# A two-layer transformer kernel: combining, gathers and routing of the last stage in another order, key weights folded into the query weights, and a straight TensorE program

## The reference, cut to what matters

```python
x = _layernorm(x + _L0_ffn_ref(...))           # its gather and sum are the "combine" of stage C
# layer 1, attention
Q = X @ W_q + b_q;  K = X @ W_k + b_k;  V = X @ W_v + b_v
A = softmax(einsum('bsd,btd->bst', Q, K) * scale, axis=2)
x = _layernorm(x + einsum('bst,btv->bsv', A, V))
# layer 1, feed-forward: 8 small experts, 2 of them per row, from the better of 2 groups
scores = sigmoid(xf @ gate.T);  sfc = scores + corr_bias
group_scores = top_k(sfc.reshape(N, 2, 4), 2)[0].sum(-1)     # sum of the two largest of four
sfc = sfc masked to the better group;  sel = top_k(sfc, 2)[1]
top_scores = scores[sel] / (scores[sel].sum(-1) + 1e-20)
lat = xf @ fc1_w.T
out_e = relu2(lat @ w1[e].T) @ w2[e].T;  comb = sum over e of out_e * top_scores
shared = relu2(xf @ up_w.T) @ down_w.T
x = _layernorm(x + comb @ fc2_w.T + shared)
```

## Time and profile before

| | before |
|---|---|
| time, median of 3 runs | 2147.3 us (2143.82 to 2147.42) |
| time of the profiled execution | 2149.05 us |
| its span (first to last record) | 2147.3 us |
| mean granted TensorE clock | 0.948 of full speed |
| busy of the span: PE, DVE, ACT, POOL | 90%, 67%, 41%, 33% |
| stage C: first q product of the 8 batches | 825.21, 987.93, 1151.72, 1318.39, 1483.74, 1649.88, 1816.66, 1978.68 us |

### The profile page before, as it was taken

The page is one execution under the profiler, slowest core; times in us unless marked ns, Lnnn a source line. Parts: engine busy times, 40 slices in busy tenths (PEclk is TensorE's granted clock), DMA queues, the critical chain, the costliest instruction groups (busy, mean ns, idle before and its releaser), DMA issues.

```text
span 2147.3 us, 36004 instructions
## 1 busy us (share of the span) xinstructions
PE 1926.1 (90%) x11720; PEld 1685.6 (79%) x11752; DVE 1433.3 (67%) x3448; ACT 880.3 (41%) x1580; POOL 707.5 (33%) x611
## 2 busy tenths in 40 slices
PE   7999899259999957999999999999999989989997
PEld 6888787249999956878888878877877977978976
DVE  4778887434434535786785785785786786687666
ACT  3344444232323314345344444344444434444433
POOL 4145555510000022253253254244145145145033
PEclk9999899679999987999999999999999999999999
DMA  4322222032223321021121111112112112111011
GB/s 148 152 96 96 95 97 65 25 118 79 88 78 109 114 93 42 29 80 48 33 80 41 40 62 59 38 42 80 32 48 81 30 50 81 26 55 50 11 40 60
DMA packets 92613, 144.54 MB, mean 67 GB/s; under 512 B 14543, under 2 KB 72743, under 8 KB 91569
## 3 DMA queue, kind: packets, MB, share of 16 engines
q1 hardware_dynamic: 79120, 110.99, 15.2%
q0 software_dynamic: 13344, 31.64, 5.4%
HBM read 103.21 MB, written 48.79 MB: 71 GB/s over the span
## 4 chain that ended last, share of the span: by engine, by line
PE 38%; DVE 13%; issue 6%; ACT 3%; POOL 2%; DVEq 0%; DMA 0%; ACTq 0%; POOLq 0%
PE c_ps L118 8%; PE c_ps L120 8%; PE c_ps L119 8%; PE c_ps L127 3%; PE c_ps L128 3%; PE c_ps L129 2%; PE c_ps L1693 2%; POOL c_place L1283 2%; DVE c_shared_place L1618 2%; DVE c_key L97 1%; DVE c_tmp L97 1%; PE c_ps L1754 1%; DVE c_place L1538 1%; PE c_ps L1756 1%; PE c_ps L1755 1%
## 5 line engine op out<-in xcount | busy, mean ns | idle before, releaser
L1283 POOL TENSOR_TENSOR c_place<-c_shared_place,c_place 128x512 fp32r<-128x512 f32 x256 | 328.6, 1307 | 387.7 <-DVE c_shared_place L1618 228.5
L118 PE MATMUL c_ps<-c_place 128*128 128x256 f32 (+1 forms) x768 | 250.8, 327 | 6.1 <-DVE c_place L1538 6.1
L1274 POOL DMA_INDIRECT c_gathered<-expert_results,c_slots x112 | 112.6, 1006 | 417.1 <-DVE c_pre L1467 396.8
L120 PE MATMUL c_ps<-c_place 128*128 128x256 f32 (+1 forms) x768 | 245.3, 319 | 0.0
L119 PE MATMUL c_ps<-c_place 128*128 128x256 f32 (+1 forms) x768 | 244.5, 318 | 0.0
L1618 DVE SCALAR_TENSOR_TENSOR c_shared_place<-c_ps,c_shared_place 128x512 f32<-128x512 f32 x256 | 170.1, 682 | 31.7 <-ACT c_shared_place L1413 31.6
L127 PE MATMUL c_ps<-c_downT_hi,c_place 128*128 128x256 f32 x512 | 152.8, 298 | 18.6 <-POOL c_place L1283 18.6
L118 PEld LDWEIGHTS c_ps<-c_place 128*128 128x128 f32 x768 | 146.1, 190 | 18.0 <-DVE c_place L1538 7.9
L1421 ACT ACTIVATE c_place<-c_shared_place 128x512 fp32r<-128x512 f32 x128 | 80.3, 630 | 188.9 <-DVE c_shared_place L1618 187.9
L120 PEld LDWEIGHTS c_ps<-c_place 128*128 128x128 f32 x768 | 146.0, 190 | 11.0
L119 PEld LDWEIGHTS c_ps<-c_place 128*128 128x128 f32 x768 | 146.3, 190 | 10.4
(11 more groups left out here) (345 smaller groups left out, 5638.1 us busy)
## 6 DMA issues: line engine op xcount, KB each, us to landing
c_x2T<-score_rows SPq DMA_DIRECT2D x64, 512.0 KB, 5.3
a_xT_raw<-xT SPq DMA_DIRECT2D x8, 1024.0 KB, 6.5
a_x_rows<-x SPq DMA_DIRECT2D x8, 1024.0 KB, 5.1
x_rows<-a_x SPq DMA_DIRECT2D x8, 1024.0 KB
c_pre<-x_rows SPq DMA_DIRECT2D x8, 1024.0 KB, 5.5
out<-c_x SPq DMA_DIRECT2D x16, 512.0 KB, 3.0
expert_rows<-a_zeros POOLq DMA_DIRECT2D x7, 1024.0 KB, 14.3
b_win_raw<-w_in SPq DMA_DIRECT2D x7, 1024.0 KB, 7.8
```

What stands on the lines that cost most here:

```text
L118: pe.matmul(out, lh, rh, start=(j == 0), stop=False)
L120: last = pe.matmul(out, ll, rh, start=False, stop=(j == len(terms) - 1))
L1274: pool.indirect_dma_start(rows[:, a, :], None, d["ys"], bass.IndirectOffsetOnAxis(ap=slots[:, a, t:t + 1], axis=0), bounds_check=TRASH + P ...
L1283: pool.tensor_tensor(hid_lo[:, place, :], square[:, place % RING, :], f32(hid_hi[:, place, :]), ALU.subtract).then_inc(hid_split, 1)
```

## The change

In **stage C** the key product goes: `Wq·Wkᵀ` is made once, ahead of the batches, and called `wqk`; `q` is then `x·wqk`, and `score` multiplies it with the rows `x2T` themselves. The part of the key bias that does not cancel in the softmax comes out of two extra columns of `v` (258 instead of 256) as `row_bias`, one small DVE operation for each `v` unit (line 1575 of the kernel after) and another behind each maximum (line 1584). A `v` unit now takes two banks. The next batch's combining moves from the attention into the part of the expert units. `GATHER` goes from 2 to 4, and POOL issues four tiles' gathers at the start of its batch and the other four between its splits of the first half. The route chain has 27 operations instead of 31, two of them without a wait. `gate 0` and `gateT 0` stand one `mix` earlier, `mix 7` and `ln3 1` stand behind `up (0, 0)` and `up (0, 1)`, and `x3T 1` behind `expert (0, 0)`. ACT's copies `norm_x2` stand in the last two expert units. TensorE's loop over batches 1 to 6 becomes a Python loop: its program is written out six times, and the other engines' loops stay. In **stage A** `slots` moves to the end of the list. In **stage B** `wq` and `wk` are not loaded or split there any more; they are loaded at the start of stage C. Cut to its core, the diff is:

```diff
-             ("proj", 1), ("logitT", 0), ("vk", 0), ("vk", 1), ("q", 0), ("q", 1), ("mixT", 1), ("q", 2), ("slots", 0), ("q", 3),
-             ("split", 0), ("copy", 0), ("proj", 2), ("proj", 3)]
+             ("proj", 1), ("logitT", 0), ("vk", 0), ("vk", 1), ("q", 0), ("q", 1), ("mixT", 1), ("q", 2), ("q", 3),
+             ("split", 0), ("copy", 0), ("proj", 2), ("proj", 3), ("slots", 0)]
...
-             ("score", 7), ("mix", 5), ("turn", 6), ("x3T", 0), ("combine", 4), ("mix", 6), ("turn", 7), ("gate", 0), ("combine", 5),
-             ("gateT", 0), ("mix", 7), ("ln3", 1), ("latent", 0), ("up", (0, 0)), ("scoreT", 0), ("combine", 6), ("norm3", 1),
-             ("combine", 7), ("up", (0, 1)), ("ln2", 0), ("x3T", 1), ("expert", (0, 0)), ("gate", 1), ("expert", (0, 1)), ("gateT", 1),
-             ("comb", 0), ("up", (1, 0)), ("scoreT", 1), ("out", 0), ("latent", 1), ("up", (1, 1)), ("ln4", 0), ("expert", (1, 0)),
...
+             ("latent", 0), ("up", (0, 0)), ("mix", 7), ("scoreT", 0), ("up", (0, 1)), ("ln3", 1), ("norm3", 1), ("combine", 0),
+             ("expert", (0, 0)), ("x3T", 1), ("combine", 1), ("gate", 1), ("expert", (0, 1)), ("combine", 2), ("combine", 3), ("gateT", 1),
+             ("comb", 0), ("combine", 4), ("up", (1, 0)), ("combine", 5), ("scoreT", 1), ("out", 0), ("latent", 1), ("combine", 6),
+             ("up", (1, 1)), ("combine", 7), ("ln2", 0), ("ln4", 0), ("expert", (1, 0)), ("expert", (1, 1)), ("comb", 1),
+             ("x2T", 0), ("x2T", 1), ("out", 1)]
...
+    V_COUNT = {"q": 1, "v": 2, "mix": 1, "turn": 2, "x3T": 2, "gate": 1, "gateT": 1, "scoreT": 1, "latent": 1, "x2T": 2, "comb": 1, "out": 2}
...
-    GATHER = 2
+    GATHER = 4
...
+            GATHER_AFTER = {2: (4,), 6: (5,), 7: (6, 7)}
...
-                    gather(b + 1)
+                    gather(b + 1, range(GATHER))
...
+                        if h == 0 and e in GATHER_AFTER and not end:
+                            gather(b + 1, GATHER_AFTER[e])
...
+                sums = key0[:].rearrange("p t (g e) -> p (t g) e", g=GROUPS)
+                larger = key1[:].rearrange("p t (g e) -> p (t g) e", g=GROUPS)
+                marks, pairs, win = group_m[:].rearrange("p t g -> p (t g)"), GSIZE // 2, group_n[:, :, 0]
+                chain.then(v.tensor_tensor, larger[:, :, 0:pairs], groups[:, :, 0:pairs], groups[:, :, pairs:GSIZE], ALU.max)
+                chain.step(v.tensor_tensor(sums[:, :, 0:pairs], groups[:, :, 0:pairs], groups[:, :, pairs:GSIZE], ALU.add))
+                chain.then(v.tensor_tensor, sums[:, :, pairs], larger[:, :, 0], larger[:, :, 1], ALU.add)
+                chain.then(v.tensor_reduce, marks, sums[:, :, 0:pairs + 1], AX.X, ALU.max)
+
+                chain.then(v.tensor_tensor, win, group_m[:, :, 0], group_m[:, :, 1], ALU.is_ge)
+                chain.then(v.tensor_tensor, choice[:, :, 0:GSIZE], choice[:, :, 0:GSIZE], across(win, GSIZE), ALU.mult)
+                chain.step(v.scalar_tensor_tensor(choice[:, :, GSIZE:EXPERTS], across(win, GSIZE), 0.5, choice[:, :, GSIZE:EXPERTS], ALU.is_lt, ALU.mult))
...
                     elif kind == "v":
-                        split_lo(unit, 0, v_hi[:, 2 * j:2 * j + 2, :].rearrange("p t c -> p (t c)"), v_lo[:, 2 * j:2 * j + 2, :].rearrange("p t c -> p (t c)"))
+                        banks, two = ps[:, v_bank(unit):v_bank(unit) + 2, :], slice(2 * j, 2 * j + 2)
+                        hi_n[0] = hi_n[0] + 1
+                        v.wait_ge(hi_done, hi_n[0])
+                        v.tensor_scalar(row_bias[:, two], banks[:, :, C], bias_kk[:, 0:1], None, ALU.add).then_inc(row_bias_done, 1)
+                        v.tensor_tensor(v_lo[:, two, :], banks[:, :, 0:C], f32(v_hi[:, two, :]), ALU.subtract).then_inc(v_free, 2)
                     elif kind == "score":
                         bank = s_bank(unit)
                         v.wait_ge(s_full, s_upto(b, unit, 1))
-                        v.tensor_reduce(neg_max[:, j:j + 1], ps[:, bank:bank + 2, :].rearrange("p a n -> p (a n)"), AX.X, ALU.max, negate=True).then_inc(max_done, 1)
+                        v.tensor_reduce(neg_max[:, j:j + 1], ps[:, bank:bank + 2, :].rearrange("p a n -> p (a n)"), AX.X, ALU.max, negate=True).then_inc(max_found, 1)
+
+                        v.wait_ge(row_bias_done, TILES // 2 * b + j // 2 + 1)
+                        v.wait_ge(max_found, TILES * b + j + 2)
+                        v.scalar_tensor_tensor(shift_s[:, j:j + 1], neg_max[:, j:j + 1], row_bias[:, j:j + 1], row_bias[:, j:j + 1], ALU.subtract, ALU.add).then_inc(max_done, 1)
                     elif kind == "turn":
...
-                    if kind in ("q", "k"):
-                        w_hi, w_lo = (wq_hi, wq_lo) if kind == "q" else (wk_hi, wk_lo)
+                    if kind == "q":
                         h, p = j // CH, j % CH
-                        if (kind, j) == ("q", CH):
+                        if j == CH:
                             pe.wait_ge(v_free, PROLOGUE if is_first(b) else v_upto(b - 1, ("x2T", 1)))
-                        product(pe, v_open(pe, b, unit), [(w_hi[:, c, bass.ts(p, P)], w_lo[:, c, bass.ts(p, P)], x2T_hi[:, c, bass.ts(h, HALF)], x2T_lo[:, c, bass.ts(h, HALF)])
+                        product(pe, v_open(pe, b, unit), [(wqk_hi[:, c, bass.ts(p, P)], wqk_lo[:, c, bass.ts(p, P)], x2T_hi[:, c, bass.ts(h, HALF)], x2T_lo[:, c, bass.ts(h, HALF)])
                                                           for c in range(CH)]).then_inc(v_full, 1)
                     elif kind == "v":
-                        out = v_open(pe, b, unit)
-                        for t in (2 * j, 2 * j + 1):
-                            last = product(pe, out[:, bass.ts(t % 2, C)],
-                                           [(x2T_hi[:, c, bass.ts(t, P)], x2T_lo[:, c, bass.ts(t, P)], wv_hi[:, c, :], wv_lo[:, c, :]) for c in range(CH)])
-                        last.then_inc(v_full, 1)
+                        for g in range(2):
+                            t = 2 * j + g
+                            product(pe, v_open(pe, b, unit, g)[:, 0:WIDE],
+                                    [(x2T_hi[:, c, bass.ts(t, P)], x2T_lo[:, c, bass.ts(t, P)], wv_hi[:, c, :], wv_lo[:, c, :]) for c in range(CH)]).then_inc(v_full, 1)
                     elif kind == "score":
 
-                        pe.wait_ge(v_free, v_upto(b, ("k", 3)))
+                        pe.wait_ge(v_free, v_upto(b, ("q", 2 * (j // HTILES) + 1)))
                         for h in range(2):
-                            product(pe, s_open(unit, h), [(q_hi[:, c, bass.ts(j, P)], q_lo[:, c, bass.ts(j, P)], k_hi[:, c, bass.ts(h, HALF)], k_lo[:, c, bass.ts(h, HALF)])
+                            product(pe, s_open(unit, h), [(q_hi[:, c, bass.ts(j, P)], q_lo[:, c, bass.ts(j, P)], x2T_hi[:, c, bass.ts(h, HALF)], x2T_lo[:, c, bass.ts(h, HALF)])
                                                           for c in range(CH)]).then_inc(s_full, 1)
                     elif kind == "turn":
...
-            with pe.Fori(1, BATCHES - 1) as b:
+            for b in range(1, BATCHES - 1):
                 body(b, False)
```

156 lines of the change are left out of this document (90 added, 66 removed).

## The result

The kernel after takes 2171.4 us (median of 4 runs, 2162.5 to 2174.4) against 2147.4 before (median of 4). The ratio is 1.0107, with a 95% interval of 1.0075 to 1.0139: slower by 1.1%, where a gain of 0.6% was forecast. The profiled execution is the fastest of the four, 2162.5 us, with a span of 2160.7.

A forecast was written before the change was run, and what follows sets the result against it. PE was taken to bound stage C, with DVE close behind. The terms, -44.8 - 29.0 + 12.8 - 53.3 + 54.2 + 51.5 - 4.9, gave -13.5 us and a median of 2134 us, 8-in-10 range 2095 to 2172.

The forecast's parts named there:

- outcome "slower": Whole kernel: a time above 2151.5 us, made up of rivals (a) and (c); chance 0.34.
- Terms 1: Stage C: the key product's 24 matmuls, 5.60 us in each of 8 batches, go from PE's path; -44.8 us.
- Term 3: Stage C attention: `v` in two banks makes `turn 0` wait 1.6 us for `v 2`'s split, times 8; +12.8 us.
- term 4: Stage C first half: without combinings on DVE, PE waits less from `mix 5` through expert 1; -53.3 us.
- Term 5: Stage C, `gate 1`: new PE wait of 4.65 us for DVE's split of `x3T 1`, plus lower clock; +54.2 us.
- term 6: Stage C second half: five combinings and `ln2` on DVE delay expert 4 by 7.35 us, times 7; +51.5 us.
- term 2: Stage C batch starts: PE without its 5 jumps loses their idle and the lower clock behind; -29.0 us.
- Term 7: Stage A: `slots` last lets the layernorm's part go first, and the loop exit loses less; -4.9 us.
- Rival (a): Stage C second half: POOL blocks both additions of every combining, 3.3 us each; 2158 us; chance 0.30 with other DVE losses.
- (b): Stage C: DVE keeps up, waits at `gate 1` and expert 4 shrink; 2050 us, half of it 2092; chance 0.18.
- (d): Whole kernel: the moves cancel, time within 4.3 us of before; chance 0.10.
- (c): Stage C batch starts: the 3 us gap belongs to the batch's start, not PE's jump; 2163 us; chance 0.04.

The follow-up runs named there:

- experiment 6: Kernel before with PE's and DVE's loops over batches 1 to 6 both written out: 2125.0 us, ratio 0.9892.
- experiment 1: Kernel after with DVE's loop over batches 1 to 6 written out too: 2149.1 us, ratio 1.0008.
- experiment 5: Kernel before with PE's loop over batches 1 to 6 written out, DVE's kept: 2121.8 us, ratio 0.9881.
- experiment 2: Kernel after with PE's hardware loop over batches 1 to 6 put back: 2184.2 us, ratio 1.0176.
- Experiment 7: Kernel after with the eight combinings back in the attention, all gathers at POOL's batch start, and DVE's loop written out: 2107.7 us, ratio 0.9815.
- Experiment 9: Kernel after with `gate 1` moved behind `expert (0, 1)` and `gateT 1` behind `comb 0`, combinings unmoved: 2140.4 us, ratio 0.9967.
- experiment 3: Kernel before with only `slots` moved to the end of stage A's list: 2137.5 us, ratio 0.9953.
- experiments 8: On top of Experiment 7, `gate 1` moved behind `expert (0, 1)`, `ln2` ahead of `comb 0`, nearby units reordered: 2069.6 us, ratio 0.9643.
- experiment 4: Kernel after with the eight combinings back in the attention and all gathers issued at the start of POOL's batch: 2127.8 us, ratio 0.9912.

## Why the prediction was wrong, step by step

The direction was wrong: 2134 forecast, 2171 measured, just inside the range of 2095 to 2172 and with the outcome "slower" at 0.34. Terms 1, 3, 4 and 5 were right in mechanism and nearly in size, term 6 in mechanism; terms 2 and 7 were not. Terms 1, 3 and 4 are read from traces; no run takes one of them back alone. Per batch of the loop, as forecast and as the trace of the fifth batch shows it:

| term | forecast | measured | from |
|---|---|---|---|
| 1, key product | -5.6 | -5.5 | `q` to score 14.03 in experiment 6, 8.49 in experiment 1 |
| 2, PE's jump | -5.8 | -5.3 alone | experiment 5, 26.6 / 5 |
| not forecast: DVE's jump | 0 | +3.9 | `v` piece 6.76 against 2.9; 19 of the 22 us of experiment 1 |
| 3, `v` in two banks | +1.6 | +1.6 | wait 1.48, and 0.1 in the next |
| 4, first half | -6.9 | -6.2 | -8.03 (33.52 to 25.49) and -0.77 at expert 1; set off 1.58 for the two `x3T` that left the stretch and the 0.98 that `x3T 0` now waits |
| 5, `gate 1` | +6.95 | +6.0 | +6.02 (21.20 to 27.22); 0.77 at expert 1 added back, 0.79 for `x3T 1` taken off |
| 6, second half | +7.35 | +10.1 | 29.40 to 38.09, 17.73 to 19.14 |
| sum | -2.4 | +4.6 | batch 166.14 to 170.81 |

**The failed step is term 2,** -29.0 forecast, some -13 measured here. Its text said that PE's 5 jumps cost 29.0 and that batch 7, which has no gap, proves it. Both hold, in the kernel before: experiment 5 gives 26.6. What failed is that I asked only of PE. The other engines kept their loops, and I took no account of what DVE does behind its jump: it is late at its first two splits, by 1.7 and 2.2 us. Before, PE's own pause and the key products lay over that. In the kernel after, both covers are gone at once, `v 0` now takes the banks of `q 0` and `q 1`, and PE waits 2 us and runs 16 matmuls at the lower clock. Experiment 1 takes back 22 us, experiment 2 shows that PE's straight program is worth only 13 here. With term 6 it makes the sign: neither alone brings the measured 24 us. For this term I never asked what stood behind the other engines' jumps, nor what hid it. The sentence on the Trainium skill's figure for a branch ("Advanced Engine Details and Errata", section Control Flow Timing: some 108 ns) stands as it did: the traces show 3 us on PE and about 4 on DVE in all, far above it, and the trace decides.

**Term 6 was sized too low, by 2.7 of 10.1 us.** From `comb 0` to the square that frees expert 4's bank I added up 36.75, and DVE took 37.94 (1596.03 to 1633.29 + 0.68), 1.2 more. The combinings cost nearly what I had said: three of the six had an operation of 1.4 us beside POOL's subtraction (below), three had none. Route was 1.1 longer: its first operation, 0.16 in the earlier trace rows, took 1.87 beside a gather and a subtraction of POOL, and 1.85 to 1.87 in all six batches of the loop. The other 1.3 is the clock: behind the second wait, 2.23, the 12 down matmuls of expert 4 took 2.92 in place of 1.62, where my sum had ended. The first wait, 3.54, costs as much behind expert 0, but that lies under the second wait. The rows are those of combine 2, of POOL beside it, and of the route's first operation:

```profile
1596.17 0.48 DVE L1492 SCALAR_TENSOR_TENSOR c_pre<-c_gathered,c_gates,c_pre 128x256 f32<-128x256 f32 x1
1596.68 1.40 DVE L1494 SCALAR_TENSOR_TENSOR c_pre<-c_gathered,c_gates,c_pre 128x256 f32<-128x256 f32 x1
...
1596.40 1.41 POOL L1300 TENSOR_TENSOR c_place<-c_shared_place,c_place 128x512 fp32r<-128x512 f32 x1 [0.84 <-ACT c_place L1442]
...
1599.83 1.87 DVE L1525 TENSOR_SCALAR c_expd<-c_expd 128x32 f32<-128x32 f32 x1
```

The rule of the Trainium skill that spoke against this change ("SBUF — State Buffer", section Who interferes with whom) is borne out in its form (1.40 with POOL at work, 0.48 without) but not to the length of rival (a): of the two additions one waits, not both. In the three dear combinings of the fifth batch the first addition starts 0.1 to 0.2 us before POOL's subtraction and runs at its own length, while POOL's takes 1.41 to 1.52 instead of 1.29; the second addition then waits for POOL. Both waited in 2 of 56 combinings. Rival (a) had read the earlier trace rows as three blocked operations of four; they show two, 1.39 and 1.06. The route's first operation has one SBUF input, so the rule as the prediction put it does not cover it, and it waited longest. Experiment 7, with the same additions where POOL does not subtract, has none that waits: 485 ns in the mean where the kernel after has 812.

**Term 5 was right in the wait:** 4.65 forecast, 4.53 seen. The clock behind it was 1.1 (`gate 1`'s six matmuls 2.52 for 1.39), where I had taken 2.3. Experiment 9 takes that wait away by order alone. **Term 3** (1.6 forecast, 1.48 seen) and **term 4** (waits of 1.2 left at expert 1; 0.83 seen) were right.

**Term 7 was wrong in the other direction:** -4.9 forecast, -10 by the medians of experiment 3 (6 to 14) and about -15 in the traces (stage B begins at 436.9 in the mean of nine executions with the new stage A, at 451.6 in three with the old one). The term counted only the end of the stage and the exit of its loop, and nothing for the waits of 3.05 us in five of its batches, which I took for the loop's jump. They are DVE's: `find_slots` stood ahead of the split that PE waits for.

In sum: stage C was forecast 43 us too low (5 x 3.9 for DVE's jump, 7 x 2.7 for term 6, the rest in smaller differences such as the wait of `x3T 0`), and stage A 5 to 10 too high. Rival (a) named the right side and nearly the right time, 2158, by a mechanism that the runs did not show. Rivals (b) and (d) were not seen, and (c) is refuted: no "issue" wait is left at the batches' starts.

## What to carry to other kernels

A loop's jump can be a pause on any engine that has the loop (here on PE and DVE; ACT's first copy starts 1.6 us behind the first `q` in batches 1 to 7 alike), and one engine's pause can hide another's: write out the loop on the engine that bounds the kernel, then look at the first instructions of the next engine behind its own jump. Work moved to an engine with slack must be put where that engine has slack in the order of its queue, not in the mean: the same eight combinings cost 44 us less beside the scores than among the experts. A product that stands directly behind the transposes whose split it reads (here `gate 1` behind `x3T 1`) wants a unit in between: that took the whole wait away in experiments 8 and 9, and in 9, where DVE was full, a third of it came back elsewhere.

## What the runs showed of the hardware

DVE pauses behind its jump by 1.7 to 1.9 us, and with the new body by a second pause of 2.1 to 2.4 us; written out, both vanish, and with them 23 of 64 packets on queue q14. What decides on the second pause stays open. PE's own jump was 3.0 us of idle in the kernel before and 4.0 in the same loop with the new body. Behind a wait of 1.99 us PE was granted 0.53 of full speed for the next 3.5 us, so it cost 3.9; the prediction had reckoned with that only behind waits above 3 us. The length of the wait alone does not decide: behind waits of 2.05 and 2.07 in the same trace, and behind one of 3.23 in experiment 4 (at 1237.55 us), the granted clock stayed at 1.00, while behind another of 3.23 there (at 1402.43) it was 0.61 for 3 us. What decides is not shown. POOL's subtraction of 128x512 (1.29 us alone) and DVE's additions with two SBUF inputs held one another up: 1.40 for 0.48 on DVE, 1.41 to 1.52 on POOL. And stage A's length varies from trace to trace: stage B began between 428.7 and 441.9 us in the traces of nine kernels with the same stage A, which is more than most of the differences looked for here; stage lengths from a trace tell them apart where total times don't.
